# A decoder layer on one core: the causal mask in sixteen 32x32 passes, reordered turns, and a rebuilt start

## The reference

```python
def decoder(x, ctx, pos):
    z = layernorm(x); q, k, v = heads(z @ Wq.T), heads(z @ Wk.T), heads(z @ Wv.T)
    s = rope(q) @ rope(k).T / sqrt(32)
    x = x + merge(softmax(where(causal, s, -inf)) @ v) @ Wo.T
    z = layernorm(x); k2, v2 = split(ctx @ Wkv)
    w = softmax(axial_rope(z @ Wq2, pos) @ axial_rope(k2, pos).T / sqrt(16))
    x = x + merge(w @ v2) @ Wout + bout
    z = layernorm(x)
    g = z @ ((wq_gate - 128) * s_gate).T; u = z @ ((wq_up - 128) * s_up).T
    return x + (silu(g) * u) @ ((wq_down - 128) * s_down).T
```

## Time and profile before

| | |
|---|---|
| runs | 1823.09 us median of 3 (1822.44 to 1823.45) |
| profiled execution | 1822.44 us, of it span 1820.7 us |
| PE busy | 1693.9 us, 93% of the span |
| PEld | 1376.9 us |
| DVE | 1158.4 us, 64% |
| ACT | 964.3 us, 53% |
| POOL | 480.6 us, 26% |
| first mask pass of a sequence, first and last | 44.3 and 1222.85 us |
| feed-forward begins on PE | 1304.20 us |

### The profile page before, as it was taken

How to read it: one execution, slowest core, us unless ns; L and a number is a source line. 1 busy time by engine, 2 the same in 40 slices (tenths; PEclk the granted TensorE clock), 3 DMA queues, 4 the chain that set the end, 5 groups by cost and what they waited for, 6 DMA issues and landing times. The chain is left out here.

```text
span 1820.7 us, 36475 instructions
## 1 busy us (share of the span) xinstructions
PE 1693.9 (93%) x12704; PEld 1376.9 (76%) x12736; DVE 1158.4 (64%) x2143; ACT 964.3 (53%) x3791; POOL 480.6 (26%) x470
## 2 busy tenths in 40 slices
PE   4799999999999999999999999997899999999997
PEld 2577777777777777777777777776688888888885
DVE  4677777777777777777777777765564343444432
ACT  4366666666666666666666666665542222222221
POOL 1233333333334333343333333333001110110111
PEclk8899999999999999999999999998799999999999
DMA  5010110000101001010010100101332101110110
GB/s 194 15 32 19 32 46 28 33 28 28 50 28 33 28 28 50 28 33 28 28 50 28 33 28 28 36 29 58 107 107 70 69 0 69 69 59 10 69 46 24
DMA packets 55094, 80.93 MB, mean 44 GB/s; under 512 B 4880, under 2 KB 25488, under 8 KB 55056
## 3 DMA queue, kind: packets, MB, share of 16 engines
q1 hardware_dynamic: 55056, 80.43, 13.6%
HBM read 63.63 MB, written 16.78 MB: 44 GB/s over the span
## 5 line engine op out<-in xcount | busy, mean ns | idle before, releaser
L652 ACT ACTIVATE prob<-bank,nmax 128x128 f32<-128x128 f32 x1536 | 537.3, 405 | 108.3 <-DVE nmax L833 108.3
L652 ACT ACTIVATION_READ_ACCUMULATOR prob<-bank,nmax 128x1 f32 x1536 | 377.5, 246 | 0.0
L833 DVE TENSOR_REDUCE nmax<-bank 128x4 f32<-128x512 f32 x384 | 241.2, 684 | 97.0 <-PE bank L478 70.9
L1109 PE MATMUL fbank<-shared,piece_hi 128*128 128x512 f32 x1152 | 280.3, 394 | 0.0
L1109 PEld LDWEIGHTS fbank<-shared,piece_hi 128*128 128x128 f32 x1152 | 215.8, 187 | 53.2
L382 POOL TENSOR_TENSOR rope_buf<-rope_buf 128x512 f32<-128x512 f32 x128 | 165.2, 1291 | 300.3 <-DVE rope_buf L790 300.0
L456 PE MATMUL bank<-shared,z1T_h 128*128 128x512 f32 x768 | 204.3, 409 | 5.1 <-DVE shared L947 3.8
L443 PE MATMUL bank<-ident,prob 128*128 128x128 f32 x1536 | 191.9, 278 | 10.9 <-ACT prob L652 10.9
L1261 DVE SCALAR_TENSOR_TENSOR h<-fbank,su_c,sil 128x512 f32<-128x512 f32 x88 | 66.0, 750 | 206.1 <-PE fbank L1109 199.0
L443 PEld LDWEIGHTS bank<-ident,prob 128*128 128x128 f32 x1536 | 174.8, 143 | 20.5 <-ACT prob L652 16.5
L659 ACT ACTIVATE probT<-bank 128x512 f32<-128x512 f32 x192 | 115.3, 600 | 130.9 <-PE bank L443 130.8
(11 more groups left out here) (156 smaller groups left out, 2921.3 us busy)
## 6 DMA issues: line engine op xcount, KB each, us to landing
xA<-in_x SPq DMA_DIRECT2D x32, 256.0 KB, 2.9
xB<-in_x SPq DMA_DIRECT2D x32, 256.0 KB, 2.8
x_scratch<-x SPq DMA_DIRECT2D x32, 256.0 KB, 2.0
shared_loaded<-x_scratch SPq DMA_DIRECT2D x8, 1024.0 KB, 7.7
xr<-x_scratch SPq DMA_DIRECT2D x8, 1024.0 KB, 5.6
out<-xr SPq DMA_DIRECT2D x8, 1024.0 KB, 4.3
cx<-in_ctx SPq DMA_DIRECT2D x32, 128.0 KB, 2.2
range_window<-in_wg SPq DMA_DIRECT2D x27, 112.0 KB, 2.0
```

What stands on the lines that cost most here:

```text
L652: last = nc.scalar.activation(prob[:, c, i, :], S[c][:, i * P:(i + 1) * P], ACT.Exp, bias=nmax[:, c, i:i + 1], accum_out=rs[:, h:h + 1])
L833: nc.vector.tensor_reduce(out=nmax[:, c, :], in_=S[c][:, :].rearrange("p (g k) -> p g k", g=G), op=ALU.max, axis=AX, negate=True).then_inc ...
L1109: last = nc.tensor.matmul(dst[:, :], w[:, k, cols], z[:, k, :], start=(n == 0), stop=(n == len(passes) * KT - 1))
```

## The change

Four things change together.

1. **The mask.** POOL builds another pattern: in the 32 rows of row group r the array `causal[row, j, key]` holds the mask of query 32 j + row. `scores1` adds it in sixteen passes: for each column group j and row group c a 32x32 identity and 32 rows of mask, 512 columns wide (four heads read the same 128), into bank c, output partitions 32 j to 32 j + 31.
2. **Turns of the loop.** On PE the transposes of k1 stand ahead of `transpose_prob("2b")`, the k2 projection stands behind the transposes of q1, and `attend2("2b")` stands ahead of the transposes of `rbc2`. The copy kT1 goes from DVE to ACT. On DVE the rotary products of k2 move behind `row_maxima("2b")`. ACT takes the exponentials of bank 0 ahead of the copy rT2.
3. **The start.** The first layer norm comes ahead of the rotary angles; `first_projections` on PE does q, k and v of sequence 0 with waits on high and low parts apart; kv2 is loaded ahead of o1; q2 and o2 are split later.
4. **The first turns.** In the turn of sequence 0, q1 of sequence 1 and k2 are projected ahead of `transpose_prob`, and on DVE and POOL the steps follow.

```diff
@@ pool, mask
-            pool.affine_select(out=causal[:, :, :], in_=causal[:, :, :], compare_op=ALU.is_ge, fill=NEG,
-                               base=0, pattern=[[0, G], [-1, P]], channel_multiplier=1).then_inc(c_ready, 1)
+            for r in range(G):
+                rows = slice(32 * r, 32 * (r + 1))
+                pool.wait_ge(c_ready, r + 1)
+                pool.affine_select(out=causal[rows, :, :], in_=causal[rows, :, :], compare_op=ALU.is_ge, fill=NEG,
+                                   base=0, pattern=[[32, G], [-1, P]], channel_multiplier=1).then_inc(c_ready, 1)
+            pool.wait_ge(c_ready, G + 1)
...
@@ pool, turn
+                if is_first(nx):
+                    rope_sum("q1", nx)
+                    rope_sum("k1", nx)
+                if is_first(sq):
+                    split_ctx(sq)
+                    rope_sum("q1", nx)
+                    rope_sum("k2", sq)
...
@@ tensor, scores1
-                for c in range(G):
-                    nc.tensor.matmul(S[c][:, :], ident_b[:, :], causal[:, :, :].rearrange("p g k -> p (g k)"),
-                                     start=True, stop=False, skip_group_check=True)
+                for j in range(G):
+                    for c in range(G):
+                        rows = slice(32 * c, 32 * (c + 1))
+                        nc.tensor.matmul(S[c][32 * j:32 * (j + 1), :], ident_b[rows, rows], causal[rows, j, :].unsqueeze(1).to_broadcast([32, G, P]),
+                                         start=True, stop=False, skip_group_check=True)
...
@@ tensor, turn
+                if is_first(nx):
+                    first_projections()
+                    return
...
+                if is_first(sq):
+                    pe.wait_ge(v1_r, 1)
+                    transpose_z1(1)
+                    project_q1(nx)
+                    pe.wait_ge(cxT_lo, 1)
+                    project(PB, cxT_h, cxT_l, "kv2", CKT, slice(0, D), fresh=True).then_inc(pj["k2"], 1)
                 if has_o:
+                    attend2("2b")
                     pe.wait_ge(rb_r[2], oq + 1)
...
                     transpose4(TC, columns(rbc2[:, :, :].rearrange("p h d -> p (h d)"))).then_inc(ri_d[2], 1)
-                    attend2("2b")
...
+                if has_s and has_c:
+                    pe.wait_ge(cxT_lo, sq + 1)
+                    pe.wait_ge(riT_r[1], sq + 1)
+                    project(TC, cxT_h, cxT_l, "kv2", CKT, slice(0, D)).then_inc(pj["k2"], 1)
...
-                if has_c:
-                    transpose_prob("2b", cq)
                 if has_n:
                     pe.wait_ge(rot["k1"], nx + 1)
                     transpose4(PA, columns(RA["k1"])).then_inc(rT_d["k1"], 1)
+                if has_c:
+                    transpose_prob("2b", cq)
...
@@ scalar, turn
+                if has_s:
+                    exponentials("1", sq, (0,))
                 if has_o:
                     act.wait_ge(ri_d[2], oq + 1)
                     nc.scalar.activation(rT2[:, :], TC[:, :], ACT.Copy).then_inc(riT_r[2], 1)
                 if has_s:
-                    exponentials("1", sq)
+                    exponentials("1", sq, (1, 2, 3))
...
+                if has_n:
+                    act.wait_ge(rT_d["k1"], nx + 1)
+                    nc.scalar.activation(flat(kT1), (TC if is_first(nx) else PA)[:, :], ACT.Copy).then_inc(rT_r["k1"], 1)
...
@@ vector, turn
+                if is_first(sq):
+                    z1T_low(1)
+                    split_low(["kv2"])
+                    rope("q1", nx, PA, DK1, cos1, sin1, DK1 ** -0.5)
+                    first_copies()
...
                 if is_first(sq):
-                    split_low(["o1", "kv2"])
+                    rope("k2", sq, PB, DK2, *axial(sq), 1.0)
+                    split_low(["o1"])
...
-                    rope("k2", sq, TC, DK2, *axial(sq), 1.0)
...
                 if has_c:
                     row_maxima("2b", cq, range(G))
+                if has_s and has_c:
+                    rope("k2", sq, TC, DK2, *axial(sq), 1.0)
                 if has_s:
                     normalise(2, x1A, z2, sq)
-                if is_first(sq):
-                    split_low(["q2", "o2"])
...
-                if has_n:
-                    dve.wait_ge(rT_d["k1"], nx + 1)
-                    nc.vector.tensor_copy(flat(kT1), PA[:, :]).then_inc(rT_r["k1"], 1)
...
@@ vector, start
             dve.wait_ge(x_in, 16)
             statistics(1, xA, 0)
             normalise(1, xA, z1, 0)
+            rotary_angles()
+            split_low(EARLY[:1])
             z1T_low(0)
-            split_low(EARLY)
+            split_low(EARLY[1:2])
+            rotary_table()
```

More of the change, by code:

```diff
@@ L414, in turn @@
                     spread(1, sq, rinv1, rbc1, H1, DK1)
-                    split_ctx(sq)
+                    if cq is not None:
+                        split_ctx(sq)
                 if cq is not None:
@@ L422, in turn @@
                     ctx_low(1, sq)
-                if nx is not None:
+                if nx is not None and cq is not None:
                     rope_sum("q1", nx)
                 if sq is not None:
-                    rope_sum("k2", sq)
                     rough_rstd(2, sq)
-                if nx is not None:
+                    if cq is not None:
+                        rope_sum("k2", sq)
+                if nx is not None and sq is not None:
                     rope_sum("k1", nx)
@@ L569, in turn @@
                     attend1()
[L570 to L572 removed]
+                if has_n and has_c:
+                    project_q1(nx)
                 if has_s:
[L574 to L576 removed]
                     pe.wait_ge(cn_r[1], sq + 1)
@@ L642, in z1T_high, with exponentials @@
                 nc.scalar.activation(flat(z1T_h), PC[:, :], ACT.Copy).then_inc(zT_hi[1], 1)
-            def exponentials(u, q):
+            def exponentials(u, q, banks=range(G)):
                 rs = (rsum1, rsum2)[kind(u) - 1]
-                if u != "2b":
+                if u != "2b" and 0 in banks:
                     wait(act, ri_r[kind(u)], q)
-                for c in range(G):
+                for c in banks:
                     act.wait_ge(nmax_r[kind(u)], G * nth(u, q) + c + 1)
@@ L843, in z1T_low, with row_sums, first_copies @@
                 low(z1T_l, PC[:, :], z1T_h, zT_lo[1])
+            def row_sums(q):
+                dve.wait_ge(p_r[1], G * (q + 1))
+                wait(dve, rb_r[1], q)
+                nc.vector.reciprocal(rinv1[:, :], rsum1[:, :]).then_inc(ri_r[1], 1)
+            def first_copies():
+                row_sums(0)
+                even_copies("1", 0)
             def axial(q):
@@ L876, in turn @@
                     normalise(1, xA, z1, nz)
[L877 to L880 removed]
+                if has_s and has_c:
+                    row_sums(sq)
                     even_copies("1", sq)
@@ L927, in turn @@
                     even_copies("2b", cq)
-                if has_n:
-                    dve.wait_ge(rT_d["k1"], nx + 1)
-                    nc.vector.tensor_copy(flat(kT1), PA[:, :]).then_inc(rT_r["k1"], 1)
-                if nz is not None:
+                if nz is not None and has_s:
                     z1T_low(nz)
@@ L950, in _, with rotary_angles, rotary_table @@
             LOOP_STEPS = 8
+            def rotary_angles():
+                pos_t = pos_sb[:, :].rearrange("p (b c) -> p b c", c=2)
+                full_s = ang_s[:, :].rearrange("p (b c i) -> p b c i", b=B, c=2)
+                turns = turns_sb[:, :]
+                dve.wait_ge(pos_in, 16)
+                for i in range(HALF):
+                    last = nc.vector.tensor_scalar(full_s[:, :, :, i], pos_t, float(np.float32(10000.0 ** (-i / HALF))), None, ALU.mult)
+                link(last)
+                link(nc.vector.tensor_scalar(turns, ang_s[:, :], 1.0 / TWO_PI, MAGIC, ALU.mult, ALU.add))
+                link(nc.vector.tensor_scalar(turns, turns, MAGIC, None, ALU.subtract))
+                for part in (PI_A, PI_B, PI_C):
+                    link(nc.vector.scalar_tensor_tensor(out=ang_s[:, :], in0=turns, scalar=-part, in1=ang_s[:, :],
+                                                        op0=ALU.mult, op1=ALU.add))
+                link(nc.vector.tensor_scalar(ang_s[:, :], ang_s[:, :], math.pi - 1e-6, -(math.pi - 1e-6), ALU.min, ALU.max))
+                link(nc.vector.scalar_tensor_tensor(out=ang_c[:, :], in0=ang_s[:, :], scalar=-1.0, in1=ang_s[:, :],
+                                                    op0=ALU.mult, op1=ALU.max))
+                nc.vector.tensor_scalar(ang_c[:, :], ang_c[:, :], -1.0, math.pi / 2, ALU.mult, ALU.add).then_inc(tab, 1)
+            def rotary_table():
+                dve.wait_ge(tab_act, 2)
+                flat_s = ang_s[:, :].rearrange("p (b j) -> p b j", b=B)
+                flat_c = ang_c[:, :].rearrange("p (b j) -> p b j", b=B)
+                c2 = cos2[:, :, :].rearrange("p b (j e) -> p b j e", e=2)
```

(5 more changed lines are left out.)

111 lines of the change are left out of this document (56 added, 55 removed).

## The result

The changed kernel takes 1826.13 us (median of 8 runs, 1825.72 to 1831.45) against 1822.18 us (8 runs) of the kernel before on the same chip: ratio 1.0028, 95% interval 1.0017 to 1.0039. It is slightly slower. 1799 was predicted.

What follows compares the result with a forecast made beforehand. PE's attention phase, with its 38.13 us loop turns, was taken as the bound. Loop -3, start -18.8 and end -1.3 sum to -23 on the profiled 1822.4: 1799 us, own range 1789 to 1808, 62%.

Steps and rivals of the forecast that it cites:

- What bounds the kernel, the turn up to scores 2b: Attention loop: PE nearly always at work, turn 38.13 us; in the new order scores 2b come 26.44 us after the z1 transposes.
- the wait for k1: Loop, PE ahead of the k1 transposes: a new wait of 1.17 us, released by POOL's sum.
- the small steps, z2 and the range reduction 1.85: DVE in the loop behind the maxima of 2b: 1.85 us of the 9.38 from scores 2b to the k1 transposes.
- the -0.1 us a turn: Loop turn: from 38.13 to 38.0 us, error perhaps 0.2; -3 us over 30 turns.
- The mask worth nothing: Start of each loop turn: sixteen passes take 0.3 to 0.96 us, and the wait for rbc hides the gain, worth 0.
- the rival of sixteen passes one after the other: Mask in each loop turn: passes do not overlap, 2.8 us more a turn, 1882 us in all; chance 9%.
- The start: Start and turn of sequence 0: -16.4, +2.4 and -4.8 sum to -18.8 us, bounds -12 to -23.
- -16.4: Start: first maxima at 29.9 instead of 46.28 us, bound by DVE's layer norm of sequence 1.
- +2.4: Turn of sequence 0: x1 comes 23.7 us after the maxima instead of 21.3, as POOL's widening stands later.
- The -4.8: Turn of sequence 0, x1 to next maxima: 12.4 instead of 17.2 us, with two splits moved behind the k1 products.
- The end: Last turns: attend2 moves into the last cross-attention's 3.01 us wait for rbc; after small costs, -1.3 us in all.
- the PE-bound case: Loop: the wait for k1 does not come, a turn takes 36.8 us, 1764 in all; chance 15%.

## Why the prediction was wrong

- **What bounds the kernel, the turn up to scores 2b:** right to 0.1 us, and the wait for k1 that the change brings is there, released by POOL's sum as forecast.
- **"the small steps, z2 and the range reduction 1.85":** this step failed. I took the 1.85 from the earlier trace rows, where POOL idles 5.50 us ahead of its sum, but the same edit put the sum of k2 beside exactly these steps. It measured 2.74 (675.46 to 678.20), of which the third step took 1.04 instead of 0.16 beside that sum. With the two kept apart and no new wait the turn is 37.90 and the time 1799.75 us. The term was mis-sized by 0.88 us, in 27 turns 24 us of the 27 by which 1799 missed. That this kernel then lands on the forecast's 1799 is partly luck: its start gives 2.7 us less than forecast, its loop 3 us more (a turn is 37.90, not 38.0). I also chose the -0.1 us a turn with "an error of perhaps 0.2", far too narrow for a chain on which one more engine had started to work.
- **The mask worth nothing:** the size of a pass was right (0.37 us, in the range 0.3 to 0.96), nearly all of it is hidden in the changed loop (0.08 a turn), and the rival of sixteen passes one after the other is out. But "nothing" was reached by arithmetic on waits alone. In the kernel before, the same mask costs 6.8 us, since the wait behind it grows and the clock falls in some turns. Two readings of the earlier trace rows were off, though nothing in the sum hangs on them. The first mask pass has no record there, so the wait for kT1 was about 0.34 us and not 0.55. And the 0.74 us from mask to scores are not three even spacings: the single records stand 0.215 us apart, and the scores start 0.31 after the last, so some 0.1 us does lie at the change of mode. The changed kernel has the same 0.31 there. Its additional change, ahead of the mask, costs nothing that can be seen: the mask starts 1.15 us behind the z1 transposes with either mask.
- **The start:** -16.4 and +2.4 came as -16.7 and +3.0 (24.3 instead of 21.3). The -4.8 failed: it came as -1.1 (16.1 instead of 17.2), because I moved the splits out of the way of the k1 products and did not ask who stood behind them: the kT2 copies, and PE's z2 transposes with them. Nor did I ask who ran beside them: the sum of k1 on POOL, 3.24 us long instead of 1.26, and through it the second split, 1.07 us longer. This is the step that failed in the loop once more. Moving the copies ahead, which also ends that meeting, brought 2.9 of the missing 3.7 back.
- **The end:** forecast -1.3, measured -0.3. The wait for rbc shrank by 1.2 us, but rbc itself came 2 us later relative to the mask.
- **The rivals:** the PE-bound case (1764, turn 36.8) was not what this change is, but it is what its loop can be: 1770 and 36.93 with the k2 products in DVE's idle time. None of the rivals had a loop turn longer by 0.65.

## What to carry to other kernels

A duration that was read while a neighbour engine was idle holds only as long as that neighbour stays idle: when a move puts GpSimd work beside VectorE steps on the critical chain, list what each of the two reads from SBUF and price the step at the end of the other's instruction. Of work that is moved within an engine's chain, look first whether it fits into that engine's wait ahead of the chain; the same two products cost 1.2 us behind the maxima, and ahead of them they delayed the maxima by 0.2. And work taken off a busy PE ahead of a wait does not shorten the turn, it lengthens an idle stretch, and with 1.4 us of it the clock fell in 5 of the 31 turns here.

## What the hardware showed that was not expected

- One VectorE step of one element per partition, normally 0.16 us, takes 1.04 beside a GpSimd sum that started 0.27 us before, and ends with it. The step with one tensor input takes 0.21 beside the same sum.
- It works the other way round too. In the turn of sequence 0 of the changed kernel GpSimd's sum of k2, elsewhere about 1.3 us long, took 3.24 beside a split on VectorE that had started 0.17 us earlier; first VectorE's row, then GpSimd's:

```profile
40.95 2.28 DVE L994 TENSOR_TENSOR w_o_lo<-w_o_lo_loaded,w_o_hi 128x2048 fp32r<-128x2048 f32 x1
```

```profile
41.12 3.24 POOL L388 TENSOR_TENSOR rope_buf<-rope_buf 128x512 f32<-128x512 f32 x1 [2.04 <-DVE rope_buf L822]
```

- Sixteen 32x32 passes of 512 columns, on all row and column groups at once, are through in 0.37 us at full clock (to the start of the scores), against 0.95 for the four full passes; a second set of sixteen adds 0.21 (0.58 us for 32).
- Behind an idle stretch of 1.4 us in an otherwise busy turn the granted clock fell to 0.50 in 5 of 31 turns, behind one of 1.16 us in none, and behind one of 1.83 us in two turns of one kernel and in none of another. What decides in which turns it does was not settled.
